# Experts rounded to half blocks: 36 blocks of 128 rows in place of 39 in the first and the last mixture of experts

## The reference

```python
scores = softmax(x @ router_w); weights, idx = top_k(scores, 2)      # L0; L3 takes the softmax over the two
gate, up = x @ gate_proj[e], x @ up_proj[e]                          # 256 -> 704 (L0), 256 -> 512 (L3)
out[token] += weight * ((silu(gate) * up) @ down_proj[e])            # 704 or 512 -> 256
```

## Time and profile before

| | us |
|---|---|
| median of 3 runs | 1708.04 |
| profiled execution, its own time | 1703.92 |
| span of the profiled execution | 1702.0 |
| PE busy | 1483.9 (87%) |
| DVE busy | 945.4 (56%) |
| ACT busy | 536.4 (32%) |
| POOL busy | 472.2 (28%) |

### The profile page before, as it was taken

One profiled execution on the slowest core, in us unless ns is written; L12 is line 12 of the kernel. 1 busy time (PEld: TensorE's weight loads), 2 busy tenths in 40 slices (PEclk: granted clock), 3 DMA queues, 4 the chain that ended last, 5 costly groups with the idle time before them and its releaser, 6 DMA issues. The chain is left out here.

```text
span 1702.0 us, 33505 instructions
## 1 busy us (share of the span) xinstructions
PE 1483.9 (87%) x11960; PEld 1123.9 (66%) x11961; DVE 945.4 (56%) x2428; ACT 536.4 (32%) x1143; POOL 472.2 (28%) x517
## 2 busy tenths in 40 slices
PE   5887899999979986799988999668888888899995
PEld 3664799999967853455545555346566665699995
DVE  4556244444438967766646533589986466322221
ACT  2331111111137745455532256233331333011010
POOL 0102344444410002111112232423111010466663
PEclk9999999999988998899998999879999999999998
DMA  4209777777720005434305122210000005588885
GB/s 145 47 2 294 237 209 233 210 231 209 230 60 1 2 2 160 136 88 113 89 23 184 38 87 83 70 31 19 1 1 1 1 2 192 165 244 236 232 241 148
DMA packets 127860, 199.85 MB, mean 117 GB/s; under 512 B 20224, under 2 KB 77312, under 8 KB 127552
## 3 DMA queue, kind: packets, MB, share of 16 engines
q1 hardware_dynamic: 107104, 169.15, 30.6%
q0 software_dynamic: 20640, 29.16, 8.3%
HBM read 165.71 MB, written 34.64 MB: 118 GB/s over the span
## 5 line engine op out<-in xcount | busy, mean ns | idle before, releaser
L1576 DVE TENSOR_REDUCE l1a_nm<-l1a_sc 128x1 f32<-128x512 f32 (+3 forms) x256 | 107.2, 483 | 53.6 <-PE l1a_sc L1712 53.6
L2454 ACT ACTIVATE e0b_sg<-e0b_gp 128x640 f32<-128x640 f32 x78 | 33.5, 481 | 263.3 <-PE e0b_gp L2394 263.3
L2367 POOL DMA_INDIRECT y_sum<-e0b_yb,e_token x39 | 63.2, 1620 | 140.4 <-DVE e0b_yb L2481 137.4
L2454 ACT ACTIVATE e3b_sg<-e3b_gp 128x512 f32<-128x512 f32 x39 | 23.3, 598 | 191.9 <-PE e3b_gp L2394 191.9
L2367 POOL DMA_INDIRECT y_sum<-e3b_yb,e_token x39 | 62.7, 1608 | 61.7 <-DVE e3b_yb L2481 58.7
L1710 PE MATMUL l1a_sc<-l_stack_k,l_stack_q 128*128 128x512 bf16 (+3 forms) x256 | 58.9, 308 | 17.0 <-PEq L1354 15.1
L1710 PEld LDWEIGHTS l1a_sc<-l_stack_k,l_stack_q 128*128 128x128 bf16 x256 | 25.3, 99 | 61.0 <-issue 27.0
L2473 DVE TENSOR_TENSOR e0b_hT<-e0b_up,e0b_sg 128x640 f32<-128x640 f32 x39 | 32.2, 825 | 57.8 <-PE e0b_up L2394 57.8
L2762 POOL TENSOR_TENSOR f_hq<-f_q,f_q 128x704 f32<-128x704 f32 x16 | 22.9, 1433 | 136.4 <-DVE f_q L2749 136.4
L1246 DVE TENSOR_REDUCE a_nm<-a_sc 128x8 f32<-128x512 f32 x64 | 39.7, 684 | 37.1 <-PE a_sc L1096 37.1
L1471 POOL TENSOR_TENSOR xn<-xn 128x512 f32<-128x512 f32 x8 | 10.1, 1269 | 177.7 <-DVE xn L1439 177.7
(11 more groups left out here) (638 smaller groups left out, 4054.3 us busy)
## 6 DMA issues: line engine op xcount, KB each, us to landing
e3k_wgu<-in_L_ffn_W SPq DMA_DIRECT2D x40, 512.0 KB
e3b_wgu<-in_L_ffn_W SPq DMA_DIRECT2D x38, 512.0 KB, 4.9
e0k_wgu<-in_L_ffn_gate_proj SPq DMA_DIRECT2D x20, 704.0 KB, 4.2
e0k_wgu<-in_L_ffn_up_proj SPq DMA_DIRECT2D x20, 704.0 KB, 5.5
e0b_wgu<-in_L_ffn_gate_proj SPq DMA_DIRECT2D x19, 704.0 KB, 4.3
e0b_wgu<-in_L_ffn_up_proj SPq DMA_DIRECT2D x19, 704.0 KB, 5.6
x_rows<-xn SPq DMA_DIRECT2D x3, 2048.0 KB, 8.3
l_parts<-l1p_split SPq DMA_DIRECT2D x16, 384.0 KB, 3.1
```

The costliest lines, as they stand in the source:

```text
L1576: nc.vector.tensor_reduce(nm[:, g % 2, q, i:i + 1], sc[q], AX_X, ALU.max, negate=True).then_inc(max_done, 1)
L2367: pool.indirect_dma_start(y_sum, bass.IndirectOffsetOnAxis(ap=token[:, n:n + 1], axis=0), yb[n % 2][:], None, compute_op=ALU.add).then_inc ...
L2454: last = nc.scalar.activation(sg[rows, chunks, :], gp[rows, chunks, :], ACT.Silu)
```

## The change

`ROUTED` becomes the number of blocks of `HALVES = Layout(NE, 64)`: experts are rounded to 64 rows, and 32 whole and 4 mixed blocks of two halves hold any routing, 36 in all with 40 owners. e0 and e3 take the layout and the longer routing chain that e1 has. The mixed blocks are numbers 4, 13, 22 and 31 of the order in time. A mixed block has x stationary in two column tiles of 64, waits for both halves' gate and up matrices, has its hidden rows transposed on PE behind `turn_rows` of the block after the next, and its down product stands where a whole block's stands. The second half's down matrices are copied by ACT to `first_weights`, half of them behind each of two silus, ahead of time. A mixed block's result is added to `y_sum` in two sends, one for each half (the other half's rows go to spare rows), the second behind the landing of the first. There are three buffers for gate and up matrices, so that a load waits for the up product three units back, and the first two loads behind the first are issued at once. All loops are unrolled, and PE reads a block's expert into its register right in front of the down product.

```diff
-ROUTED = (TOP * B * S + NE * (P - 1)) // P
+HALVES = Layout(NE, P // 2)
+ROUTED = HALVES.blocks
...
+    ends = [(2 * i + 1) * self.full // (2 * self.mixed) if centred else (i + 1) * self.full // self.mixed for i in range(self.mixed)]
...
+            self.HELD = 3
...
                     dve.wait_ge(counted, 1)
-                    if lay is None:
-                        nc.vector.tensor_copy(cnt[:], count).then_inc(step, 1)
...
-                    else:
-                        bits = lay.unit.bit_length() - 1
+                    bits = lay.unit.bit_length() - 1
+                    nc.vector.tensor_scalar(held_i[:], count, float(lay.unit - 1), None, ALU.add).then_inc(laid, 1)
...
-                        nc.vector.tensor_copy(token[:], row_f[:]).then_inc(routed, 1)
+                        nc.vector.tensor_scalar(away[:], row_f[:, lay.full:], const("aside"), None, ALU.subtract).then_inc(laid, 1)
+                        nc.vector.tensor_copy(plan.send[:, 0:lay.full], row_f[:, 0:lay.full])
+                        nc.vector.tensor_copy(token[:, 0:NB], row_f[:]).then_inc(routed, 1)
+                        dve.wait_ge(laid, 16)
+                        nc.vector.tensor_tensor(apart[:], bcast(away[:], 2, lay.per), bcast(const("parity"), 1, lay.mixed), ALU.mult)\
+                            .then_inc(laid, 1)
+                        dve.wait_ge(laid, 17)
+                        nc.vector.tensor_scalar(plan.send[:, lay.full:], apart[:].rearrange("p m u -> p (m u)"), const("aside"), None, ALU.add)
...
                 def _(sp):
-                    plan.load_gate_up(sp, owner, 1, 1)
-                    step(0, 0)
-                    with sp.Fori(0, (NB - 3) // 2) as i:
-                        for j in (1, 0):
-                            step(i * 2 + 2 - j, j)
+                    for k in range(1, len(block_of)):
+                        if k >= plan.HELD:
+                            sp.wait_ge(up_made, block_of[k - plan.HELD] + 1)
+                        plan.load_gate_up(sp, owner, owner_of[k], k % plan.HELD)
...
                     def send(n):
                         pool.wait_ge(y_copied, n + 1)
-                        if n:
-                            pool.wait_ge(rows_summed[(n - 1) % 2], 16 * (earlier[(n - 1) % 2] + (n - 1) // 2 + 1))
-                        pool.indirect_dma_start(y_sum, bass.IndirectOffsetOnAxis(ap=token[:, n:n + 1], axis=0), yb[n % 2][:], None,
-                                                compute_op=ALU.add).then_inc(rows_summed[n % 2], 16)
+                        for i, (block_n, at, done, value) in enumerate(sent):
+                            if block_n == n:
+                                if i:
+                                    pool.wait_ge(*sent[i - 1][2:])
+                                pool.indirect_dma_start(y_sum, bass.IndirectOffsetOnAxis(ap=plan.send[:, at:at + 1], axis=0), yb[n % 2][:],
+                                                        None, compute_op=ALU.add).then_inc(done, 16)
...
+                    def product(at, chunks, dst, n, done):
+                        if is_mixed(n):
+                            for lo in range(0, chunks * P, BANK):
+                                hi = min(lo + BANK, chunks * P)
+                                for k in range(KC):
+                                    for u, unit in enumerate(units_of[n]):
+                                        rows = slice(u * HALF, (u + 1) * HALF)
+                                        last = nc.tensor.matmul(flat(dst)[rows, lo:hi], xT[n % 2][:, k, rows],
+                                                                wgu[unit % plan.HELD][:, k, at + lo:at + hi], start=(k == 0), stop=(k == KC - 1))
...
+                    def down(n):
+                        if n:
+                            pe.wait_ge(y_copied, n)
+                        own = lay.owner_at(order[n])
+                        e = pe.value_load(owner[0:1, own[0]:own[0] + 1], min_val=0, max_val=plan.E - 1)
...
                         for f in range(FC):
+                            last = nc.tensor.matmul(yp[first, :], hT[n % 2][:, f, first],
                                                     plan.wd[f // 2][:, bass.ds(e, 1), f % 2, :].rearrange("p a d -> p (a d)"),
                                                     start=(f == 0), stop=(f == FC - 1))
+                            if is_mixed(n):
+                                last = nc.tensor.matmul(yp[HALF:P, :], hT[n % 2][:, f, HALF:P], mixed_d[:, f * D:(f + 1) * D],
+                                                        start=(f == 0), stop=(f == FC - 1))
...
+                    for n in range(NB):
+                        gate(n)
+                        if n + 1 < NB:
+                            turn_rows(n + 1)
+                        if n and is_mixed(n - 1):
+                            turn_hidden(n - 1)
+                        up_product(n)
...
+                            down(n - 1)
+                    down(NB - 1)
...
                 def _(dve):
+                    for n in range(NB):
...
+                        hidden(n)
+                        if n:
+                            weigh_out(n - 1)
+                        if rounds is not None and n % 2:
+                            rounds.round(dve, n // 2)
+                    weigh_out(NB - 1)
```

More of the change, by code:

```diff
@@ L2445, in _ @@
-                    down(NB - 1, 0, expert(NB - 1))
+                    stay_busy(flat(gp)[:, 0:S], 4)
+                    turn_rows(0)
+                    for n in range(NB):
+                        gate(n)
[4 more added lines that the diff above has]
+                        up_product(n)
+                        if n == 0:
+                            if LEFT:
+                                pe.wait_ge(padded, 2)
+                            pe.wait_ge(plan.kept, plan.all_kept)
+                        else:
+                            down(n - 1)
@@ L2450, in silu @@
                         act.wait_ge(gate_made, n + 1)
-                        if positive(n):
+                        if n:
                             act.wait_ge(h_done, n)
+                        if is_mixed(n):
+                            last = nc.scalar.activation(flat(sg)[:, 0:F], flat(gp)[:, 0:F], ACT.Silu)
+                        else:
+                            for rows, chunks in PIECES:
+                                last = nc.scalar.activation(sg[rows, chunks, :], gp[rows, chunks, :], ACT.Silu)
@@ L2453, in silu, with copy_hidden @@
+                        last.then_inc(sg_done, 1)
+                    def copy_hidden(n):
+                        act.wait_ge(h_turned, mixed_at.index(n) + 1)
                         for rows, chunks in PIECES:
[L2454 to L2455 removed]
+                            last = nc.scalar.copy(hT[n % 2][rows, chunks, :], hp[rows, chunks, :])
+                        last.then_inc(h_copied, 1)
```

361 lines of the change are left out of this document (172 added, 189 removed).

## The result

The changed kernel takes 1727.9 us (median of 4 runs, 1721.6 to 1730.6) beside 1708.0 us for the kernel before. The ratio is 1.0113, with a 95% interval of 1.0095 to 1.0131. The forecast was 1685 us, with a range of 1675 to 1697. The change makes the kernel 1.1% slower. The profiled execution took 1730.14 us, with a span of 1728.2.

What follows compares the result with a forecast made beforehand. PE's work per block times the number of blocks was taken to bound e0 and e3; terms summed to -17.0 us in e0 and -6.1 in e3, together -23.1, taking the median 1708.04 to 1684.9, forecast 1685, range 1675 to 1697.

Steps and rivals of the forecast that it cites:

- the one on sends: Mixed blocks' two serial sends: landing 4.5 us, pace 4.7; e0 pays 0, e3 1.5 in waits and 2.2 at the tail.
- the 0.2 us from a landing to the next send: In the chain of sends on POOL: issuing the next send takes 0.2 us beyond the 4.5 us landing.
- Priced at 3.7 us for e3 and 0 for e0: Second sends: e3 pays 1.5 us for PE's three waits for rows plus 2.2 at the tail; e0 nothing.
- the first rival: Mixed blocks' products: the two column tiles run one after the other, 50 us in all, 1735 us, slower; chance 0.06.
- A mixed block costs: Four mixed blocks in each stage: each 1.36 us longer in e0 and 1.24 in e3, together 5.4 and 5.0 us.
- The register read: Rival, in front of down products: PE's read of the expert is exposed, up to 33 us, 1718 us, slower; chance 0.03.
- The DMA share: In e3's blocks: rises from 0.80 to 0.87 with the bytes in 36 slots, short of full; costed at nothing.
- Loads of mixed blocks: Weights in e3, within the harder-transfers rival: they come late at a DMA share near 0.9.
- the transfers in e3 bite harder: Rival: late fetches, late mixed-block weights, low clock at the first block; 2 us for three blocks, 3 at start; 1694, chance 0.13.
- heals at 0.8 us a slot: e3's chain of sends: a late chain makes up 5.52 - 4.7 = 0.8 us each slot; argued against the harder-transfers rival.
- Routing: Longer chain ahead of the blocks in e0 and e3: +1.8 us, bounds 1 and 2.6; e3 pays 1.8, e0 0.8.
- e0's cover of 1.0 us: Between routing and e0's first gate product: the wait for `w_pairs` hides about 1.0 us, so e0 pays 0.8.

Runs made afterwards that it cites:

- experiment 1: The changed kernel with one send for a mixed block instead of two, the second half's rows left out of `y_sum`: 1689.0 us, ratio 0.989.
- experiment 4: The kernel before, with one more send to spare rows at blocks 4, 13, 22 and 31 of e0 and e3: 1747.1 us, ratio 1.0225.
- 3: The changed kernel with the fetches of weights and next rows issued between a mixed block's two sends: 1717.2 us, ratio 1.0054.
- 5: The changed kernel with each send of a mixed block cut to its own 64 rows: 1715.7 us, ratio 1.0059.
- 8: The changed kernel with 64-row half sends, fetches between the two sends, a third output buffer and longer filler during routing: 1716.8 us, ratio 1.0051.
- 9: 64-row rounding in e0 alone, with half sends, fetches between and third output buffer; e3's blocks and routing as before: 1703.2 us, ratio 0.9990.
- experiment 10: The changed kernel with each load of gate and up weights issued as two halves at two times: 1715.4 us, ratio 1.0052.

## Why the prediction was wrong

**The step that failed** is the one on sends: "One lands 4.5 us after its issue", "the pace is 4.7", so that a late chain "makes up 5.52 - 4.7 = 0.8 in each slot", and for e0 "a slot of 7.72 takes two sends nearly in step: 0". Two of its numbers failed. The first is the 0.2 us from a landing to the next send. It holds between the two sends of a block (0.27), but an ordinary send leaves 0.77 us behind the landing, a quantity that the kernel before didn't show, as none of its sends beside loads waited for another. With a landing of 4.5 the pace is then 5.3, and a late chain in e3 makes up 0.2 us in a slot of 5.52, not 0.8, even if every landing is as before: a lag of 4.7 us would not be gone when the next mixed block comes nine slots later (an estimate from these rows). The second is the landing of the earlier trace rows, taken as a constant of the transfer. It belonged to a place in the slot: nearly every send of e3 before left 1.9 us behind a load. Out of that place sends took up to 8.5 us to land and 9.3 to the next send, nothing was made up, and the lag reached the fetches queued behind on POOL in 9 slots of e3, not 3. Of e0 the 0 was nearly right for PE, which waits once, but for a reason that I didn't have: the chain ran late there for more than half of the stage, and the slot's cushion took it. Priced at 3.7 us for e3 and 0 for e0, the eight second sends cost 39 us (experiment 1), about 33 in e3 and 4 in e0, and eight added to the kernel before cost the same in all (experiment 4).

Without the second sends the time was 1689. That this lies in my own range for the forecast is no merit: without its 3.7 us for sends my sum would be 1681. What experiment 1's profile has above the terms of my sum lies elsewhere: 4.1 us in the stages between, 3.3 behind e0's last down product, 2.9 up to e0's first gate product and 1.6 in that product.

**What was right.** The tiles run side by side (2.74 us for a gate product; the first rival is out). A mixed block costs 1.3 to 1.5 us more in e0 and 1.1 to 1.3 in e3; I had 1.36 and 1.24. The register read isn't exposed, since whole slots kept 7.72 and 5.52. The DMA share reached the 0.87 I gave, but only in experiment 1, and my sum for it used 39 loads where the change has 40 (0.89). Loads of mixed blocks did not come late.

**The rival that came nearest** was "the transfers in e3 bite harder", with the right place and order of events and a price of 9 us. It gave the third cause, the clock at the start, 3 us, and put the waits at three blocks. That a lag "heals at 0.8 us a slot" was its flaw too.

**Routing** is partly right. From its first product to the `found` product, the one that finds the rows, it takes 1.8 us more in both stages (22.1 against 20.3, 21.1 against 19.3), as I had. But e0's cover of 1.0 us wasn't there, and behind that product e0 and e3 take 1.0 and 0.9 us more: up to the first gate product e3 pays 2.7 us, not 1.8, and e0 2.8, not 0.8. The rest of e0's 5.0 lies ahead of the routing, in work that the change doesn't touch. I had left out that PE's idle time ahead of the `found` product grows from 3.73 to 5.57 us, behind which the product runs in a stretch with a granted clock of 0.52 and takes 2.10 us in place of 1.30. More filler only moved that stretch.

**Not foreseen:** GpSimd's longer drain, which adds 3.3 us behind e0's last down product.

**Open.** Why POOL's drain has two lengths. And the 6.7 us in the stages between, of which I had none. They are not a steady price of the change: in the fifteen profiles of kernels with 64-row rounding this stretch takes 0.3 to 7.5 us more than the 946.6 us of the one profile of before, and 1.2 us more in experiment 4, without the rounding. Two to three us of the spread are layer 2's feed-forward part, which takes 232 to 233 us on PE in ten of the seventeen profiles (before, 3 and 5, for instance) and about 235 in seven (the changed kernel, 8 and 9 among them); in 9 it has one more window of 10 us with a granted clock below 1 (0.83). No run tells what decides between the two. How much of the cost of a late send is its meeting with loads is not settled either: experiment 10 took 10 to 12 us off by moving the loads, and the 0.77 us and the some 3 us that a send takes whatever its rows would be there without them.

## What to carry to other kernels

A transfer that waits for its predecessor is a chain with a pace of its own. Before adding one link, compare chain time per slot with the slot, and take the chain's time from where the link would stand beside the large loads, not from where the old ones stand: here a landing of 4.5 us became up to 8.5, and four more links in each of two stages, most of all in the one with slots of 5.52 us, ate a saving of 40 us. Count the time from a landing to the next issue too, from a place where one really waits for the other: 0.77 us of it decided here whether a lag heals. PE at 100% busy says that it sets the end now; it does not say how near the next chain is. To price such a link, add it to the old kernel as a dummy (experiment 4): one run would have given the size of the loss ahead of the change, though not its split over the stages.

## What was not expected of the hardware

- An accumulating indirect transfer of 64 rows holds the next one back for 3.5 to 4.0 us, one of 128 rows for 4.5, without loads beside them.
- Its landing goes with its distance to loads on the other queue: in the changed kernel the median was 7.0 us in e0 and 6.2 in e3 for sends with a load's transfer issued within 1 us of them, and 4.3 and 4.1 for the others. A late chain can fall into step with the loads and stay late.
- The next transfer in such a chain left 0.77 us behind the landing, or 0.27 between the two sends of one block.
- GpSimd's drain at the end of a stage took 4.5 us with 39 blocks and 8.5 with 36, while the last transfer landed in 3.8 us in both; with one more gather it took 9.7.
- Two column tiles of 64 with 512 and 256 float32 columns run fully side by side: 16 loads and 16 products in 2.74 us, as against 2.67 for the untiled product over the same columns.
